# Two DMA orders on SyncE: last layer-two stores moved from ScalarE, mask loads paired over a third buffer

## The reference, cut to what matters

```
x = layernorm(x + L0(x, adj))      # GRU on adj @ x
x = layernorm(x + L1(x, adj))      # GCN: dinv * (adj + I) * dinv @ (x W) + b
x = layernorm(x + L2(x, adj))      # 4-head attention, masked where adj == 0
x = layernorm(x + L3(x, adj))      # hyperbolic layer, adj @ xt

# L2: q, k, v = x Wq + bq, ...      as n x 4 heads x 32
attn = einsum('nhc,mhc->hnm', q, k) / sqrt(32)
e    = where(adj == 0, 0, exp(attn - rowmax)); alpha = e / sum(e)
out  = einsum('hnm,mhc->hnc', alpha, v)
beta = sigmoid([out, x Ws + bs, out - x_r] @ Wb);  beta*x_r + (1-beta)*out
```

## Time and profile before

| | |
|---|---|
| median of 3 runs | 1846.05 us (1840.38 to 1847.43) |
| profiled execution, its own time | 1848.52 us |
| its span, first to last instruction | 1846.7 us |
| mean granted TensorE clock | 0.985 of full |
| PE, DVE, ACT, POOL busy | 95%, 68%, 52%, 49% |
| layer three, first to last unit | about 595 to 1591 us |

### The profile page before, as it was taken

The page is one execution under the profiler, slowest core; times in us unless marked ns, Lnnn a source line. Parts: engine busy times, 40 slices in busy tenths (PEclk is TensorE's granted clock), DMA queues, the critical chain, the costliest instruction groups (busy, mean ns, idle before and its releaser), DMA issues. The chain is left out here.

```text
span 1846.7 us, 40348 instructions
## 1 busy us (share of the span) xinstructions
PE 1759.7 (95%) x14992; PEld 1158.7 (63%) x14992; DVE 1255.3 (68%) x2454; ACT 959.8 (52%) x1456; POOL 898.4 (49%) x853
## 2 busy tenths in 40 slices
PE   7999999999996999999999999999999999799996
PEld 3444444444443777787778877877877777444442
DVE  4777775221216898999999989989979999201322
ACT  0110110100003888898889988988988889201101
POOL 0111110111125455788787787787877876340111
PEclk9999999999997999999999999999999999899998
DMA  9867666799987445445445444544454543797792
GB/s 374 308 224 260 249 232 244 272 379 381 381 311 242 147 150 156 145 143 172 144 148 164 145 151 141 156 154 143 153 155 150 161 145 104 283 376 278 283 328 68
DMA packets 138524, 396.91 MB, mean 215 GB/s; under 512 B 16240, under 2 KB 67184, under 8 KB 113776
## 3 DMA queue, kind: packets, MB, share of 16 engines
q1 hardware_dynamic: 115776, 353.42, 55.7%
q10 hardware_dynamic: 20016, 32.78, 4.9%
q0 software_dynamic: 2560, 8.39, 1.6%
HBM read 333.19 MB, written 61.34 MB: 214 GB/s over the span
## 5 line engine op out<-in xcount | busy, mean ns | idle before, releaser
L904 ACT ACTIVATE arena<-arena,small 128x2048 f32<-128x2048 f32 x256 | 512.4, 2002 | 0.0
L669 PE MATMUL bank<-ident,arena 128*128 128x128 f32 x3584 | 473.9, 274 | 1.2 <-ACT arena L904 0.7
L669 PEld LDWEIGHTS bank<-ident,arena 128*128 128x128 f32 x3584 | 419.4, 141 | 66.2 <-DVE arena L1221 2.7
L535 PE MATMUL bank<-arena,stat_s 128*128 128x512 f32 x1008 | 444.7, 598 | 9.3 <-DMA arena<-adj_cols 5.2
L916 ACT ACTIVATE arena<-bank 128x512 f32<-128x512 f32 x624 | 351.1, 596 | 119.2 <-PE bank L669 116.1
L642 PE MATMUL bank<-k,parts 128*128 128x512 f32 x1024 | 371.2, 444 | 35.1 <-DMA parts<-q_dram 15.4
L535 PEld LDWEIGHTS bank<-arena,stat_s 128*128 128x128 f32 x1008 | 191.2, 192 | 237.9 <-issue 236.5
L692 PE MATMUL bank<-arena,stat_x 128*32 128x128 f32 x8192 | 278.0, 276 | 3.8 <-DMA arena<-group_dram 3.7
L692 PEld LDWEIGHTS bank<-arena,stat_x 128*32 128x32 f32 x8192 | 208.6, 110 | 59.6 <-issue 48.0
L535 PE MATMUL bank<-arena,stat_x 128*128 128x512 f32 x512 | 228.8, 598 | 11.0 <-DMA arena<-adj_cols 8.8
L642 PEld LDWEIGHTS bank<-k,parts 128*128 128x128 f32 x1024 | 154.8, 190 | 97.5 <-issue 40.3
(11 more groups left out here) (155 smaller groups left out, 1434.1 us busy)
## 6 DMA issues: line engine op xcount, KB each, us to landing
arena<-adj_cols SPq DMA_DIRECT2D x190, 1024.0 KB, 6.8
arena<-adj SPq DMA_DIRECT2D x64, 512.0 KB, 5.4
stat_s<-adj SPq DMA_DIRECT2D x64, 512.0 KB, 5.1
group_dram<-stat_s SPq DMA_DIRECT2D x64, 512.0 KB, 3.1
arena<-group_dram SPq DMA_DIRECT2D x256, 128.0 KB, 2.8
k_dram<-arena ACTq DMA_DIRECT2D x32, 256.0 KB, 7.2
q_dram<-arena ACTq DMA_DIRECT2D x32, 256.0 KB, 11.6
k<-k_dram POOLq DMA_DIRECT2D x32, 256.0 KB, 8.8
```

Of the source, the lines that this page charges most:

```text
L535: mm_ = pe.matmul(bank[:, to, :], stat[:, jt, :], ring[:, s, j, :], start=(jt == 0), stop=(jt == TILES - 1))
L669: last = pe.transpose(bank[:, b_, h * P:(h + 1) * P], cols[:, st % SETS, h, u * P:(u + 1) * P], ident[:, :])
L904: act.activation(cols[:, s_, h, :], cols[:, s_, h, :], ACT.Exp, bias=shift[:, t % 2, 1, i:i + 1], scale=-1.0, accum_out=blocksum[:, t % 2, ...
```

## The change

- The last chunk's k, q and root stores leave ACT and go to SP's list, placed between the first mask loads. SP also takes the loading back of the last chunk's k from POOL (`gcn_k4_last_in`); the load for the chunk before stays on POOL with a semaphore of its own (`gcn_k4_sixth_in`).
- ACT's exp and ln table load moves ahead of the last chunk of layer two.
- There are three mask buffers. The load of mask g may start when POOL has done mask g-3. Masks are loaded 8 ahead, and both mask loads of a set stand ahead of `store_group`.
- The third buffer takes two more chunks' place in `stat_s`: four chunks' `xt` go by way of DRAM. `store_xt` stands ahead of `load_group`.
- Queries are loaded in the even sets, one set sooner.

```diff
--- before.py
+++ after.py
@@ -58,8 +58,9 @@
 SCORE_LEAD = 13
 EXP_LEAD = 4
 BIAS_LEAD = 6
-MASK_AHEAD = 7
-SPILLED = (4, 5)
+MASK_AHEAD = 8
+MASKS = 3
+SPILLED = (2, 3, 4, 5)
 MIX_COLUMN = 2
 
 COPY_OUT_AT = 4
@@ -261,7 +262,7 @@
         turned = [stages[i] for i in (0, 1, 6, 7, 2, 3, 10, 11)]
         group_slots = arena[:, RING + 10 * CHUNK:RING + 12 * CHUNK]
         spilled = stat_s[:, SPILLED[0] * TPC:(SPILLED[-1] + 1) * TPC, :].rearrange("p t f -> p (t f)")
-        adj_in = (arena[:, RING + 4 * CHUNK:RING + 6 * CHUNK], spilled[:, 0:2 * CHUNK])
+        adj_in = (arena[:, RING + 4 * CHUNK:RING + 6 * CHUNK], spilled[:, 0:2 * CHUNK], spilled[:, 2 * CHUNK:4 * CHUNK])
         tail = stat_s[:, TILES - 2 * TPC:TILES, :].rearrange("p t f -> p (t f)")
         blocks = [tail if len(group) == 2 else spilled[:, 2 * CHUNK:3 * CHUNK] for group in GROUPS]
         maskbias = [half_[:, i * BLOCK:(i + 1) * BLOCK] for half_ in
@@ -311,13 +312,13 @@
         gcn_pe, gcn_act, gcn_dve, gcn_pool = [sem(f"gcn_{e}") for e in ("pe", "act", "dve", "pool")]
         gcn_x1_in, gcn_x2_out, gcn_root_out = sem("gcn_x1_in"), sem("gcn_x2_out"), sem("gcn_root_out")
         gcn_k_out, gcn_q_out = sem("gcn_k_out"), sem("gcn_q_out")
-        gcn_k4_in, gcn_k4_last_in = sem("gcn_k4_in"), sem("gcn_k4_last_in")
+        gcn_k4_in, gcn_k4_sixth_in, gcn_k4_last_in = sem("gcn_k4_in"), sem("gcn_k4_sixth_in"), sem("gcn_k4_last_in")
         CP = Steps("turned", "x2_turned", "k", "q", "vs")
         CA = Steps("agg", "x2_t", "k_hi", "q_hi")
         CV = Steps("self", "dinv", "y", "bn6", "bn", "x2", "k_lo", "q_lo", "v", "root")
         CG = Steps("x1_bias", "eps", "rstd")
 
-        adj_landed = [sem(f"adj_landed{s}") for s in range(2)]
+        adj_landed = [sem(f"adj_landed{s}") for s in range(MASKS)]
         q4_landed = [sem(f"q4_landed{s}") for s in range(2)]
         bias_ready = sem("bias_ready")
         scores_ready = sem("scores_ready")
@@ -389,12 +390,13 @@
                 load_ring(1, c, False)
 
 
-            def load_mask(c, m, fresh):
+            def load_mask(c, m):
                 t, b = m // BLOCKS, m % BLOCKS
-                if not (fresh and m < 2):
-                    sp.wait_ge(bias_ready, c * COLS + m - 1)
-                sp.dma_start(adj_in[m % 2], adj[bass.ds((c * TPC + t) * P, P), b * BLOCK:(b + 1) * BLOCK]
-                             ).then_inc(adj_landed[m % 2], 16)
+                g = c * COLS + m
+                if g >= MASKS:
+                    sp.wait_ge(bias_ready, g - MASKS + 1)
+                sp.dma_start(adj_in[g % MASKS], adj[(c * TPC + t) * P:(c * TPC + t + 1) * P, b * BLOCK:(b + 1) * BLOCK]
+                             ).then_inc(adj_landed[g % MASKS], 16)
 
             def load_queries(c, t, fresh):
                 if not (fresh and t < 2):
@@ -429,18 +431,18 @@
             def load_mask_ahead(c, n):
                 ahead = c * COLS + n + MASK_AHEAD
                 if ahead < CHUNKS * COLS:
-                    load_mask(ahead // COLS, ahead % COLS, False)
+                    load_mask(ahead // COLS, ahead % COLS)
 
             def attention_loads(c):
                 for st in range(SPC):
                     g = c * SPC + st
                     load_mask_ahead(c, 2 * st + 0)
+                    load_mask_ahead(c, 2 * st + 1)
                     store_group(g, 0)
-                    load_group(g, 0)
-                    load_mask_ahead(c, 2 * st + 1)
                     if st == 0 and c - 2 in SPILLED:
                         store_xt(c - 2)
-                    if st % SETS == 1:
+                    load_group(g, 0)
+                    if st % SETS == 0:
                         ahead = c * TPC + st // SETS + 2
                         if ahead < CHUNKS * TPC:
                             load_queries(ahead // TPC, ahead % TPC, False)
@@ -479,14 +481,35 @@
 
 
             sp.wait_ge(gru_pe, GP(CHUNKS - 1, "y_turned"))
-            load_mask(0, 0, True)
+            load_mask(0, 0)
             sp.wait_ge(gcn_q_out, 64 * (CHUNKS - 2))
             load_queries(0, 0, True)
             sp.wait_ge(ring_multiplied, 2 * CHUNKS * SLOTS)
-            load_mask(0, 1, True)
+            load_mask(0, 1)
+            load_mask(0, 2)
             load_queries(0, 1, True)
-            for m in range(2, MASK_AHEAD):
-                load_mask(0, m, True)
+            load_mask(0, 3)
+            last = CHUNKS - 1
+            sp.wait_ge(gcn_act, CA(last, "k_hi"))
+            sp.wait_ge(gcn_dve, CV(last, "k_lo"))
+            for g in range(4):
+                sp.dma_start(k4_dram[last, g, :, :, :].rearrange("h c n -> (h c) n"),
+                             k_parts[:, g % 2, :].bitcast(F32)).then_inc(gcn_k_out, 16)
+            load_mask(0, 4)
+            sp.wait_ge(gcn_k_out, 64 * CHUNKS)
+            for g in range(4):
+                sp.dma_start(k4[g * C:(g + 1) * C, :, last * CHUNK:CHUNKS * CHUNK].bitcast(F32),
+                             k4_dram[last, g, :, :, :].rearrange("h c n -> c h n")).then_inc(gcn_k4_last_in, 16)
+            sp.wait_ge(gcn_act, CA(last, "q_hi"))
+            sp.wait_ge(gcn_dve, CV(last, "q_lo"))
+            for g in range(4):
+                sp.dma_start(q4_dram[last, g, :, :, :].rearrange("h c n -> (h c) n"),
+                             q_parts[:, g // 2, :].bitcast(F32)).then_inc(gcn_q_out, 16)
+            load_mask(0, 5)
+            sp.wait_ge(gcn_dve, CV(last, "root"))
+            sp.dma_start(root_dram[:, last * CHUNK:CHUNKS * CHUNK], root_out).then_inc(gcn_root_out, 16)
+            for m in range(6, MASK_AHEAD):
+                load_mask(0, m)
             for c in range(CHUNKS):
                 attention_loads(c)
 
@@ -631,7 +654,8 @@
 
                 t, b = m // BLOCKS, m % BLOCKS
                 if fresh and b == BLOCKS - 1 and h == 0:
-                    pe.wait_ge(gcn_k4_last_in, 64 * (CHUNKS - LAST_BLOCK_CHUNK))
+                    pe.wait_ge(gcn_k4_sixth_in, 64)
+                    pe.wait_ge(gcn_k4_last_in, 64)
                 if b == 0 and h == 0:
                     pe.wait_ge(q4_landed[t % 2], 64 * (2 * c + t // 2 + 1))
                 if not (fresh and m == 0 and h < 2):
@@ -893,8 +917,8 @@
             with act.Fori(0, CHUNKS // 2 - 1) as pair:
                 for k, from_bank in ((1, 1), (2, 0)):
                     gcn(2 * pair + k, False, from_bank)
+            act.preload_act_table_set(EXP_AND_LN)
             gcn(CHUNKS - 1, False, 1)
-            store_projections(CHUNKS - 1)
 
 
             def exponent(c, st, h):
@@ -977,8 +1001,6 @@
                     if k in post:
                         post[k]()
 
-            act.preload_act_table_set(EXP_AND_LN)
-            store_root(CHUNKS - 1)
             for i in range(EXP_LEAD):
                 exponent(0, i // H, i % H)
             attention(0, True, False)
@@ -1465,9 +1487,10 @@
 
                 if not (first and m < 4):
                     pool.wait_ge(masked_ready, (c * COLS + m - 3) * H)
-                pool.wait_ge(adj_landed[m % 2], 16 * ((c * COLS + m) // 2 + 1))
+                g = c * COLS + m
+                pool.wait_ge(adj_landed[g % MASKS], 16 * (g // MASKS + 1))
                 pool.nop(nofuse=True)
-                pool.tensor_scalar(maskbias[m % 4], adj_in[m % 2], 0.0, MASKED, ALU.is_equal,
+                pool.tensor_scalar(maskbias[m % 4], adj_in[g % MASKS], 0.0, MASKED, ALU.is_equal,
                                    ALU.mult).then_inc(bias_ready, 1)
 
             def post_steps(c, factor_at=31):
@@ -1620,11 +1643,10 @@
             mask_bias(0, 0, True)
             add_bias(CHUNKS - 1)
             gcn_rsqrt(CHUNKS - 1)
-            load_k4(CHUNKS - 2, gcn_k4_last_in)
+            load_k4(CHUNKS - 2, gcn_k4_sixth_in)
             mask_bias(0, 1, True)
             pool.wait_ge(gcn_dve, CV(CHUNKS - 1, "root"))
             mask_bias(0, 2, True)
-            load_k4(CHUNKS - 1, gcn_k4_last_in)
             for m in range(3, BIAS_LEAD):
                 mask_bias(0, m, True)
             attention(0, True, False)
```

## The result

The changed kernel took 1856.03 us (median of 8 runs, 1852.56 to 1859.61), the kernel before 1841.02 us (median of 8, 1837.84 to 1847.43). The ratio is 1.0077, with a 95% interval of 1.0059 to 1.0095: slower, by 14 to 15 us. The profiled execution took 1858.08 us, its span is 1856.4 us.

A forecast was written before the change was run, and what follows sets the result against it. PE was taken to bound layer three (busy 960 of 990 us), DVE following at 92%. Terms -6 - 19 - 1.5 + 33.5 + 1.4 = +8.4 us on the 1846.05 median gave 1854.5; forecast 1854 us, range 1820 to 1866.

The forecast's parts named there:

- the likeliest case: Set 6 of chunks 1 to 6: PE pauses with a clock dip behind; 1846 to 1864 us, chance 0.45.
- my three chances: Whole kernel: faster by over 0.5% 0.25, slower by over 0.5% 0.34, within 0.5% 0.41.
- The pair's store: Set 6, six chunks: store waits for mask 18; 22 us of pauses plus 11.4 of clock, 33.5 lost (16 to 45).
- The store isn't late: Rival, set 6: PE would not stand for the pair, only the gains remain; 1821 us, chance 0.2.
- The pause is short or the clock doesn't fall: Rival, set 6: the pause comes without the clock's fall, or is short; 1843 us, chance 0.25.
- DVE becomes the bound: Rival, layer three: DVE gives back 10 of the queries' 19 us while the pause stands; 1864 us, chance 0.1.
- The gains: Start of layer three 6 us, queries 19 and spill store 1.5, all taken off the time.
- queries: Layer three: loaded some 15 us sooner, PE's waits for them go; gain 19 us (17 to 22).
- the spill store: Chunk 6: store issued some 10 us sooner lands before POOL asks; gain 1.5 us.
- the seam: Start of layer three: first turned unit at 587.5 against 594.80, some given back; gain 6 us (3 to 9).
- The third buffer: Mask loads: only takes away POOL's waits for masks; worth nothing unless it helps the pair's store.
- End: End of layer three: two more `load_xt` issues ahead of the first ring slot; 1.4 us lost (0 to 2).

The follow-up runs named there:

- the control: The changed kernel measured again with no edit, on the same chip as the follow-up runs: 1.0096 of the kernel before, 1858.7 us.
- e1_lead7: The changed kernel with masks loaded 7 ahead in place of 8, nothing else: 0.9891 of the kernel before, 1819.5 us.
- e2_between: The changed kernel, still 8 ahead, with the second mask load put back behind `load_group`: 0.9899 of the kernel before, 1820.6 us.
- e9_wait_new: e1_lead7 with SP waiting for mask 18 ahead of the pair's store in set 6 of chunks 1 to 6: 0.9959 of the kernel before, 1832.2 us.
- e3_queries: The kernel before with the queries loaded in the even sets, nothing else: 0.9928 of the kernel before, 1831.1 us.
- e5_two: The changed kernel with two mask buffers, masks 6 ahead and two chunks spilled: 0.9946 of the kernel before, 1832.0 us.
- e0_after: The same run as the control, the changed kernel again with no edit: 1.0096 of the kernel before, 1858.7 us.
- e4_wait: The kernel before with SP waiting for mask 18 ahead of the pair's store in set 6 of chunks 1 to 6: 1.0078 of the kernel before, 1855.6 us.
- e7_seam: The kernel before with only the seam's part (last stores and k load on SP, table load sooner): 0.9988 of the kernel before, 1840.3 us.
- e10_lead7_again: e1_lead7 measured once more, with no further edit: 0.9864 of the kernel before, 1818.1 us.

## Why the prediction was right or wrong

The forecast, a pause in set 6 of six chunks with a fall of the clock behind each, is what happened: six stops of 3.56 to 4.85 us (3 to 5 expected), each followed by a clock of 0.50 to 0.58, SP's queue held by the load that needs mask 18. 1856.03 us lies in the likeliest case's own range. Its size was short: against the 1846.05 us it started from, 1854 means 8 us up, while on equal terms the change costs 14 to 15 (18 to 19 in the control). That 1856.03 is only 2 us from 1854 is partly luck: the three runs of the kernel before that I started from have a median 5 us above that of the eight beside the changed kernel. The outcome, slower by over 0.5%, had the second of my three chances, 0.34, behind 0.41 for no change.

**The pair's store.** 33.5 us expected, 38 measured (control less e1_lead7). The pauses sum to 25.25 (22 expected) and the clock to 13.0 (11.4; 11.5 in the control). From mask 18's end to the batch it took 9.76 us in chunk 4, 9.7 to 11.1 over the six and 10.2 in the mean (9.3 expected; my own terms, 0.5, 4.6 and 4.1, make 9.2). The term that was mis-sized is the store's landing: 5.2 us in the mean, not 4.6; the loads took the rest. I had the rule right (the store needs mask 2st+6 instead of 2st+5), but costed landing behind a mask as a given. The experiments split it: waiting for POOL 14 to 17 us, the mask just in front the rest.

**Rivals.** "The store isn't late" needed PE's batch to come 8.8 us behind mask 18's end; in the changed kernel it came 4.8 to 6.9 us behind (5.4 in the mean, 5.1 expected). It is what e1_lead7 and e2_between made true: 20 and 19 us under the kernel before, where the rival had 25. "The pause is short or the clock doesn't fall" fell for the change itself, but describes e9_wait_new, where the stops were 1.7 to 3.1 us and three of six left the clock at 1.00. "DVE becomes the bound", by giving back 10 us, fell: it gave back 2.4 in e3_queries, and in e1_lead7 DVE was busy 905.25 of 960 us while PE was idle for 11.0.

**The gains.** I summed 26.5 us less 1.4 for the end, 25.1; e1_lead7 and its repetition show 20 and 25 by the ratio (20.1 and 21.7 by the medians). The pieces, each by itself on before: queries 13.3 (19 expected, and under my lower bound of 17, though the interval reaches 18), the spill store 5.2 (1.5), the seam 2.2 alone and 4.7 at the first turned unit in the changed kernel (6). The queries' term was mis-sized at its upper bound: I took PEld's 20.0 for it, and 19 lies near it, but PE itself stood only 15.4, of which 12.5 came back; with 1.7 for the clock behind the one long stop that makes 14.2, against 13.3 measured. In the seam I let the first turned unit start when k has landed; it starts when the scores on that k are done, 1.84 us later (588.28 and 590.12). k itself landed 0.8 us later than I had it: its load left at 581.46, not 580.5, and took 6.8 us to PE (7.0 expected). The first pair then cost PE 1.56 us at 610.01, close to the 1.3 in my sum (606.8 less 605.5).

**The third buffer.** Costed at nothing, "POOL is not the bound there". Over the kernel before, the runs leave little for it: the pieces without it sum to 20.7 us, less 1.1 to 2.2 for the end, and the whole is 20 to 25, so 0 to 6 us. But the reason that I gave fails under the new order. With masks paired ahead of the store, e5_two lost about 10 us against e1_lead7 with two buffers and the lead of 6 that these allow. POOL isn't the bound in the mean, but a mask that comes late holds up the small steps behind it in POOL's list, and with them ACT and PE. e5_two changes buffers and lead together; on the order of before a third buffer was not tried, so this is its worth under the new order only.

**End.** 1.4 expected. PE's wait there grew from 5.25 to 6.36 us in the changed kernel (7.45 in the control) and to 7.1 and 7.3 in e1_lead7 and its repetition: 1.1 to 2.2.

**The page's rule on a DMA's time.** In set 6, stores without a transfer right in front landed in 2.6 to 4.0 us (e9_wait_new), those 0.45 us behind one in 4.9 to 6.1 (the changed kernel). The Trainium skill's "DMA: Bandwidth & Descriptors", Anatomy of one DMA, has its fit from DMAs issued by GpSimd, while these are issued by SyncE; as an estimate for these bytes it gives 3.2 us. The case's numbers lie around that for a DMA with nothing right ahead, and well above it behind another on the same queue.

## What to carry to other kernels

In an in-order queue a prefetch costs by what it waits for, and not only by what it moves: for each load write down which event of another engine it needs, and let none that needs a later event stand ahead of a transfer that someone needs soon. A deeper prefetch with one more buffer can ask for *more*: lead +1 and two loads in front against +1 buffer left the store one mask worse, and one constant turned a loss of 15 us into a gain of 20. And look past the wait: the transfer that the wait releases leaves right ahead of the one you need, and cost here more than the wait itself.

## What was not expected of the hardware

- A 512 KB store to DRAM takes longer to land right behind another transfer. Over all of layer three, the 18 stores of the changed kernel that SP issued within 0.1 us of finishing the issue of a 512 KB load landed in 4.9 to 7.0 us; the 58 of e9_wait_new with no issue of SP in the 3 us before them landed in 2.6 to 4.8 us, median 2.85. Why some of these take 4 us and more, as in chunk 1 of e9_wait_new, is open.
- The length of a stop alone does not say whether TensorE's clock falls. Behind all fourteen stops of 3.5 us and more at set 6 (the changed kernel, e0_after, e4_wait) the granted clock of the next 4 us was 0.50 to 0.62. Shorter ones went either way: 1.00 behind 2.87 us (e9_wait_new) and 2.46 us (e4_wait), but 0.66 behind 1.76 us (e9_wait_new), and at the batch near 610 it was 1.00 behind 1.56 us in the changed kernel and 0.64 behind 1.67 us in e0_after. The same wait of 3.4 us for ACT in layer four left it at 1.00 in e1_lead7, e7_seam, e9_wait_new and e10_lead7_again and at 0.50 in the kernel before and e2_between. At set 6 a fall cost 1.4 to 2.8 us on top of the stop.
